# The causal mask of a diagonal score chunk moves from third to first matmul of its bank

## The reference, cut to what matters

```python
scores = jnp.einsum('bhqd,bhkd->bhqk', q_full, k_full) * scale
causal = jnp.triu(jnp.ones((s, s), dtype=bool), k=1)
scores = jnp.where(causal, -jnp.inf, scores)
attn = jax.nn.softmax(scores.astype(jnp.float32), axis=-1).astype(q_full.dtype)
out = jnp.einsum('bhqk,bhkd->bhqd', attn, v)
```

## Time and profile before

| what | before |
|---|---|
| median of 3 runs | 1805.91 us (1802.36 to 1807.36) |
| the profiled execution | 1806.03 us, span of its instructions 1804.3 us |
| mean granted TensorE clock | 0.976 of 2.4 GHz |
| PE matmul busy | 1608.8 us (89%) |
| DVE busy | 1220.2 us (68%) |
| ACT busy | 1026.9 us (57%) |
| attention loop | about 116 to 1328 us of the span |
| masked chunks | 256, all in the attention loop |

### The profile page before, as it was taken

One profiled execution on the slowest core, in us unless ns is written; L12 is line 12 of the kernel. 1 busy time (PEld: TensorE's weight loads), 2 busy tenths in 40 slices (PEclk: granted clock), 3 DMA queues, 4 the chain that ended last, 5 costly groups with the idle time before them and its releaser, 6 DMA issues. The chain is left out here.

```text
span 1804.3 us, 38201 instructions
## 1 busy us (share of the span) xinstructions
PE 1608.8 (89%) x14452; PEld 1318.3 (73%) x14452; DVE 1220.2 (68%) x2600; ACT 1026.9 (57%) x2017; POOL 302.1 (17%) x743
## 2 busy tenths in 40 slices
PE   3669999899999999999999999999965999988997
PEld 1357777777777777877887787787754778766886
DVE  3847766777677676777777777777746656576564
ACT  2336665666666566566666666656643435645573
POOL 3411112111211211121121121121110012020231
PEclk9879999999999999999999999999987999999999
DMA  8000000000000000000000000000011200000000
GB/s 231 1 0 2 2 2 1 2 2 1 1 2 1 2 2 2 1 1 2 2 2 1 2 2 1 2 1 2 2 26 49 81 0 1 1 19 21 1 21 27
DMA packets 27814, 23.54 MB, mean 13 GB/s; under 512 B 9692, under 2 KB 25180, under 8 KB 27508
## 3 DMA queue, kind: packets, MB, share of 16 engines
q1 hardware_dynamic: 22324, 14.77, 2.9%
q10 hardware_dynamic: 5312, 6.33, 1.2%
HBM read 19.00 MB, written 2.10 MB: 12 GB/s over the span
## 5 line engine op out<-in xcount | busy, mean ns | idle before, releaser
L697 ACT ACTIVATE pT_hi<-pT 128x512 f16<-128x512 f32 (+3 forms) x640 | 340.9, 533 | 366.7 <-PE pT L615 363.1
L818 DVE TENSOR_TENSOR pT_lo<-pT,pT_hi 128x512 f16<-128x512 f32 (+3 forms) x640 | 388.2, 607 | 159.1 <-ACT pT_hi L697 153.8
L806 DVE TENSOR_REDUCE cmx<-pS 128x1 f32<-128x512 f32 x576 | 347.9, 617 | 97.8 <-PE pS L602 94.2
L686 ACT ACTIVATE pr<-pS,nmx 128x512 f32<-128x512 f32 (+3 forms) x640 | 398.9, 623 | 11.1 <-DVE nmx L809 10.2
L615 PE MATMUL pT<-ident,pr 128*128 128x128 f32 x2176 | 346.2, 275 | 9.8 <-DVE pT_lo L818 6.9
L597 PE MATMUL pS<-lT_hi,qT_hi 128*128 128x512 f32 (+2 forms) x640 | 284.1, 444 | 57.9 <-ACT pr L686 49.0
L615 PEld LDWEIGHTS pT<-ident,pr 128*128 128x128 f32 x2176 | 258.2, 140 | 43.9 <-ACT pr L686 10.1
L657 PE MATMUL pO<-c_hi,pT_hi 128*128 128x65 f16 x2176 | 265.7, 194 | 1.2 <-DVE O L836 0.6
L658 PE MATMUL pO<-c_lo,pT_hi 128*128 128x65 f16 x2176 | 266.6, 193 | 0.0
L659 PE MATMUL pO<-c_hi,pT_lo 128*128 128x65 f16 x2176 | 263.7, 192 | 0.0
L602 PE MATMUL pS<-lT_hi,qT_lo 128*128 128x512 f32 (+2 forms) x640 | 257.4, 402 | 0.0
(11 more groups left out here) (243 smaller groups left out, 2510.0 us busy)
## 6 DMA issues: line engine op xcount, KB each, us to landing
X<-in_x SPq DMA_DIRECT2D x4, 512.0 KB, 6.8
wo<-in_w_o ACTq DMA_DIRECT2D x1, 2048.0 KB, 13.9
out<-X SPq DMA_DIRECT2D x8, 256.0 KB, 2.0
raw<-in_wd SPq DMA_DIRECT2D x14, 128.0 KB, 2.2
raw<-in_wg SPq DMA_DIRECT2D x13, 128.0 KB, 2.8
raw<-in_wu SPq DMA_DIRECT2D x13, 128.0 KB, 2.7
wqn<-in_w_qn ACTq DMA_DIRECT2D x1, 1536.0 KB, 17.6
raw<-in_qg SPq DMA_DIRECT2D x6, 128.0 KB, 2.5
```

The lines of the kernel that those rows point to most:

```text
L686: act.activation(pr[:, at % RING, 0:n * P], pS[at % 4][:, 0:n * P], ACT.Exp, bias=nmx[:, p % 4:p % 4 + 1]).then_inc(sem("exped"), 1)
L697: act.activation(pT_hi[:, a % 4, 0:chunk[a][2] * P], src, ACT.Copy).then_inc(sem("t_hi"), 1)
L806: ch.inc(dve.tensor_reduce(cmx[:, p % 2, c:c + 1], pS[at % 4][:, 0:n * P], AX.X, ALU.max))
L818: dve.tensor_tensor(pT_lo[:, a % 4, 0:w], src, pT_hi[:, a % 4, 0:w], ALU.subtract).then_inc(sem("t_lo"), 1)
```

## The change

In a diagonal chunk the mask's product is issued first and opens the bank (`start=True`); the three products that make the scores add to it (`start=False` for the first of them). In all other chunks nothing changes. The number of instructions, their operands, shapes and the semaphore on the last product are the same.

```diff
@@ scores(at)
                             w = max(256, n * P)
                             o, ks = pS[at % 4][:, 0:w], slice(c * BT, c * BT + w)
                             q_hi, q_lo = (q[:, i % 2, h * P:(h + 1) * P] for q in (qT_hi, qT_lo))
-                            pe.matmul(o, q_hi, lT_hi[:, 2, ks], start=True, stop=False)
-                            pe.matmul(o, q_hi, lT_lo[:, 2, ks], start=False, stop=False)
-                            if c == tile_at(p) // 4:
-                                pe.matmul(pS[at % 4][:, (n - 1) * P:n * P], identb[:], maskb[:], start=False, stop=False,
+                            diagonal = c == tile_at(p) // 4
+                            if diagonal:
+                                pe.matmul(pS[at % 4][:, (n - 1) * P:n * P], identb[:], maskb[:], start=True, stop=False,
                                           skip_group_check=True)
-                            pe.matmul(o, q_lo, lT_hi[:, 2, ks], start=False, stop=True).then_inc(sem("scored"), 1)
+                            pe.matmul(o, q_hi, lT_hi[:, 2, ks], start=not diagonal, stop=False, skip_group_check=diagonal)
+                            pe.matmul(o, q_hi, lT_lo[:, 2, ks], start=False, stop=False, skip_group_check=diagonal)
+                            pe.matmul(o, q_lo, lT_hi[:, 2, ks], start=False, stop=True, skip_group_check=diagonal).then_inc(sem("scored"), 1)
```

## The result

| what | before | after |
|---|---|---|
| median of the runs | 1805.66 us (4 runs) | 1786.29 us (1785.82 to 1789.15, 4 runs) |
| ratio | | 0.9898, 95% interval 0.9881 to 0.9916: 15 to 21 us less |
| the profiled execution | 1806.03 us, span 1804.3 | 1786.26 us, span 1784.5 |
| mean granted clock | 0.976 | 0.979 |

Faster, as forecast, but by 19 us and not by 12, and just outside the range (1788 to 1803). The changed kernel is one line longer, so that after line 598 all lines stand one lower; in `scores` the mask is line 599 and the three products are 601, 602 and 603.

The account below looks back on a forecast made before the run. PE was taken to bound the attention loop, with matmuls 93% of its time. Savings of 102 x 0.10 + 29 x 0.09 = 12.8 us, less 0.8, gave 1806.0 - 12 = 1794.0 us, range 1788 to 1803.

Parts of the forecast that it names:

- The mechanism: In masked chunks, a short mask product exposes the next f32 weight load; in third place the mask costs 0.12 us.
- the slower rival: At line 597, qT_hi's load starts only when the mask is through: 32 us more, 1838 us; chance 0.05.
- identb's load: Mask's weight load at the chunk's head just after a wait: 0.03 us taken; if 0.11, 1804 us, chance 0.07.
- what PE saves: Over the 256 masked chunks, PE's work shrinks by 16.3 us: 111 x 0.10 + 58 x 0.09.
- Case C: 87 masked chunks behind a wide product or transpose, no idle time between: bubble moves from line 602 to 597, nothing saved.
- the clock: Clock stays at 2.4 GHz, as PE's idle stretches grow by less than 0.1 us each.
- Case W: 111 masked chunks with PE idle before, qT_hi's load beginning only once the bank was free: 0.10 us saved each.
- case V: 58 masked chunks of one-chunk heads, right behind the last values product: 0.56 us becomes 0.47, 0.09 us saved each.
- The share that counts: Of PE's 16.3 us in the loop, 12.8 lie on the path setting its end; less 0.8 for close rivals, 12 us.
- the chain: Path followed back from the loop's last matmul through releasers: passes 102 of 111 waited chunks, 29 of 58 behind values.
- The rival that the whole sum counts: Masked chunks off the followed path count as well: 16 us less, 1790 us; chance 0.10.
- the rival of the saving turning into waiting: In waited chunks PE only waits 0.1 us longer for exponentials; 3 us less remains, 1803 us; chance 0.13.

Follow-up runs that it names:

- The two runs of the wide mask: Mask 256 columns wide instead of 128: first, on the changed kernel, 1791.36 us; third, on the kernel before, ratio 1.0004.
- the run with one-chunk heads alone: Mask first only in the 64 one-chunk heads, third in all others, against the kernel before: 1802.97 us, ratio 0.9989.

## Why the prediction was right and wrong

**The mechanism: right.** The mask leaves the load behind it exposed; where the chunk's head had a bubble already, its cost fell to 0.02 and 0.03 us (the run without a mask). The two runs of the wide mask show that it is the load, and the mask in second place that the bubble goes where the mask goes. The load of qT_hi is drawn under the mask even after a wait, so the slower rival is refuted.

**identb's load: right.** It was the one price without a row. In the waited chunks the mask ends 0.234 us (median) after its load starts; I had 0.25 at the low end and 0.33 at the high one. Two mask products in a row, each with its own load, end 0.056 us apart. The Trainium skill (TensorE: Matmul & The Clock Gate, Weight-path perf modes) lets 128 non-f32 weights load faster, and the 0.234 us of this trace agree. The Trainium skill's rule on the same page (LDWEIGHTS: columns divided by 1.2 GHz, 107 ns for 128) would by itself have put the mask's end at about 0.33 us, an estimate (0.25 us with 0.107 in place of 0.03), and the trace does not agree with it for this bf16 load.

**Two terms failed.** The first is what PE saves, above all "Case C, nothing saved"; the second is the clock, put at no change. Neither alone takes the time out of the range.

**What PE saves: too small.** I took steps from a timeline rounded to 0.01 us. Case W saved 0.108 us and not 0.10, case V 0.097 and not 0.09: 1.3 us over both. The terms given for case V, 0.07 + 0.17 + 0.24, also add up to 0.48 and not to 0.47, so that they ask for 0.08; the mask came 0.055 us behind the values and not 0.07. Worse was "Case C, nothing saved". That group was formed by whether PE's products left a gap. But in 25 of these 87 chunks the load of qT_hi had been released late though the product ahead was still running: it began 0.22 us or less ahead of that product's end, and in the others 0.27 us or more. So part of the load was already exposed. An example before (in case C by the grouping), with idle time only in the load's row:

```profile
699.82 0.40 PE L602 MATMUL pS<-lT_hi,qT_lo 128*128 128x512 f32 x1
700.02 0.19 PEld L597 LDWEIGHTS pS<-lT_hi,qT_hi 128*128 128x128 f32 x1 [0.24 <-ACT pr L686]
...
700.40 0.37 PE L602 MATMUL pS<-lT_hi,qT_lo 128*128 128x256 f32 x1
```

and the same chunk after:

```profile
688.89 0.40 PE L603 MATMUL pS<-lT_hi,qT_lo 128*128 128x512 f32 x1
689.12 0.10 PEld L599 LDWEIGHTS pS<-maskb,identb 128*128 128x128 bf16 x1 [0.28 <-ACT pr L687]
...
689.49 0.28 PE L603 MATMUL pS<-lT_hi,qT_lo 128*128 128x256 f32 x1
```

From the end of the product ahead to the chunk's end it took 0.55 us and now 0.48. In all, case C saved 2.6 us, 2.2 of it in these 25. So PE saved 20.1 us, not 16.3. With my share of 0.74 let through, that would have been 15 us less, about 1791, still inside the range.

**The share that counts: right.** I let 12 of 16.3 us through (0.74); 15.4 of 20.1 came through (0.77). By groups it fits too: the chain had 102 of 111 waited chunks, and nine tenths came through in heads of several chunks; it had 29 of 58 behind values, and 2.5 of 5.6 us came through. The rival that the whole sum counts is refuted by the run with one-chunk heads alone, and the rival of the saving turning into waiting by the waits for exponentials, which did not grow. I had not said where the rest would go; it went mostly to the turn.

**The clock: put at nothing.** I wrote that the clock stays. In the loop's body it did. But the mean granted clock varies between executions of one kernel (0.974 to 0.979 for before, with times 7 us apart), in the profiled ones at the loop's start and ahead of it, and the executions of after had more of the higher level. That makes about 4 of the 19 us, and with the 15 above it is the measured time. Whether the edit has any part in it is not shown, so that the sign of this term was chance as far as is known. My range allowed 2 us for scatter; it had to take in more on both sides.

## What to carry to other kernels

A short product costs more than its columns where the weight load behind it would otherwise be hidden under a wide product, and nearly only its columns, or less, where that load is exposed anyway: right behind a wait or behind other short products (here 0.12 us against 0.02 and 0.03). Ahead of the 4-byte transposes it cost 0.08 us, for a reason that is not shown. To place one, look for the load that is exposed already; look for it in the rows of the weight loads, not in the gaps between products. Then ask for each place whether it lies inside a chain over other engines that PE waits for later, since what is saved there comes back as idle time.

## What I had not expected of the hardware

- Doubling a bf16 mask from 128 to 256 columns in third place changed the loop by less than 0.1 us (1201.2 us both): its columns fill the time of the 4-byte load behind it.
- Transposes of 128 x 128 4-byte values run 0.109 us apart, though 128 columns at 0.46 ns are 0.06 us, and the first one ends 0.109 us behind a wide product too, whose end its load precedes by 0.26 us or more (median). With a bf16 product of 128 columns ahead it is only 7 ns later.
- A bf16 product ends 0.072 us behind a 4-byte product but 0.055 us behind another 2-byte product or a transpose (medians of the mask's end in the changed kernel, by what stands ahead). I did not test why.
- Executions of one and the same kernel differ by 7 us (1802.45 to 1809.52, before) with the mean granted clock (0.979 to 0.974).
